# A Mamba front's B and C rows: the split remainder kept in SBUF instead of PSUM, and four due times moved

## The reference, cut to what matters

```python
xc = silu(conv(in_proj(x)));  dbl = xc @ x_proj.T           # 40 columns
dt, B, C = split(dbl)                                       # 8, 16, 16
delta = softplus(dt @ dt_w.T + dt_b)
dA = exp(delta * A);  dBu = delta * xc * B
h = dA_t * h + dBu_t;  y_t = sum_n h * C_t                  # scan over 512 tokens, 16 states
out = (y + xc * D) * silu(z) @ out_proj.T
```

## Time and profile before

| | |
|---|---|
| time, median of 3 runs | 3703.71 us (3700.42 to 3713.71) |
| the profiled execution's own time | 3700.42 us |
| its span in the profile | 3699.1 us |
| PE busy | 2934.4 us (79%) |
| DVE busy | 2480.3 us (67%) |
| ACT busy | 2005.1 us (54%) |
| POOL busy | 1625.7 us (44%) |

### The profile page before, as it was taken

One profiled execution on the slowest core, in us unless ns is written; L12 is line 12 of the kernel. 1 busy time (PEld: TensorE's weight loads), 2 busy tenths in 40 slices (PEclk: granted clock), 3 DMA queues, 4 the chain that ended last, 5 costly groups with the idle time before them and its releaser, 6 DMA issues.

```text
span 3699.1 us, 42302 instructions
## 1 busy us (share of the span) xinstructions
PE 2934.4 (79%) x15540; PEld 1347.2 (36%) x15618; DVE 2480.3 (67%) x2851; ACT 2005.1 (54%) x3613; POOL 1625.7 (44%) x1005
## 2 busy tenths in 40 slices
PE   5799988956577787878776897888768888888876
PEld 2233333421222223223223633333245555555543
DVE  3887834369988887888885332877656565666552
ACT  1465651144468677767764312666545555556543
POOL 2211101124657877776875012555544444435341
PEclk6899998966678887888787997898889999999998
DMA  3222100121112211211212000011000000000000
GB/s 87 45 42 53 29 2 0 41 60 25 35 35 57 42 40 33 62 37 36 51 34 104 1 0 12 23 23 23 12 21 11 21 21 11 21 11 21 11 21 23
DMA packets 79738, 114.43 MB, mean 31 GB/s; under 512 B 16270, under 2 KB 49422, under 8 KB 78106
## 3 DMA queue, kind: packets, MB, share of 16 engines
q1 hardware_dynamic: 68268, 103.06, 11.4%
q0 software_dynamic: 11264, 8.66, 1.8%
HBM read 37.70 MB, written 17.33 MB: 15 GB/s over the span
## 4 chain that ended last, share of the span: by engine, by line
PE 46%; DVE 23%; ACT 14%; issue 7%; POOL 6%; DMA 2%; SPq 1%; POOLq 0%; DVEq 0%; ACTq 0%
DVE layer_mamba_state L1386 7%; PE psum L1166 4%; DVE psum L1374 3%; PE psum L1239 3%; ACT layer_mamba_decay L1316 3%; PE psum L2660 3%; PE psum L826 2%; PE psum L2217 2%; PE psum L958 2%; PE psum L2731 2%; PE psum L2691 2%; DVE layer_peak L767 2%; POOL layer_qk L3052 2%; ACT L1316 1%; DVE layer_v_between L2944 1%
## 5 line engine op out<-in xcount | busy, mean ns | idle before, releaser
L1428 POOL TENSOR_TENSOR layer_mamba_state<-layer_mamba_state,layer_mamba_c 128x1024 f32<-128x1024 f32 x320 | 780.9, 2459 | 351.8 <-DVE layer_mamba_state L1386 347.9
L1386 DVE TENSOR_TENSOR_SCAN layer_mamba_state<-layer_mamba_decay,psum 128x1024 f32<-128x1024 f32 x320 | 731.4, 2286 | 43.9 <-ACT layer_mamba_decay L1316 10.3
L1239 PE MATMUL psum<-layer_mamba_state,two_to_one 128*64 128x512 f32 x1280 | 420.2, 746 | 105.0 <-DVE layer_mamba_x L1403 82.9
L1316 ACT ACTIVATE layer_mamba_decay<-layer_mamba_delta_wide,layer_weights 128x511 f32<-128x511 f32 x640 | 416.2, 711 | 60.8 <-DMA layer_mamba_delta_wide<-layer_mamba_delta 30.0
L1374 DVE TENSOR_TENSOR psum<-psum,layer_mamba_u_wide 128x1024 f32<-128x1024 f32 x320 | 393.5, 1230 | 45.2 <-PE psum L1200 19.2
L767 DVE TENSOR_REDUCE layer_peak<-psum 128x2 f32<-128x1024 f32 x256 | 308.4, 1221 | 95.3 <-PE psum L738 90.6
L839 ACT ACTIVATE layer_exps<-psum 128x1024 f32<-128x1024 f32 x256 | 255.8, 1023 | 152.5 <-PE psum L806 152.5
L2851 ACT ACTIVATE layer_p<-psum,layer_stats 128x128 f32<-128x128 f32 x512 | 180.6, 369 | 136.1 <-DVE layer_stats L2973 135.9
L3057 POOL TENSOR_TENSOR layer_p<-layer_p,layer_stats 128x512 f32<-128x512 f32 x128 | 132.5, 1039 | 255.6 <-DVE layer_stats L2980 255.3
L3044 POOL TENSOR_TENSOR layer_qk<-layer_qk,layer_v_between 128x1024 f32<-128x1024 f32 x64 | 150.5, 2351 | 189.8 <-DVE layer_v_between L2944 187.9
L1326 ACT ACTIVATE layer_mamba_c<-psum 128x512 f32<-128x512 f32 x192 | 112.9, 588 | 190.5 <-PE psum L1200 187.8
(11 more groups left out here) (366 smaller groups left out, 5995.0 us busy)
## 6 DMA issues: line engine op xcount, KB each, us to landing
layer_mamba_delta_wide<-layer_mamba_delta SPq DMA_DIRECT2D x160, 128.0 KB, 2.3
layer_mamba_u_wide<-layer_mamba_work SPq DMA_DIRECT2D x160, 128.0 KB, 2.4
layer_v_between<-layer_v SPq DMA_DIRECT2D x16, 512.0 KB, 4.3
qk_dram<-layer_qk_parts SPq DMA_DIRECT2D x16, 384.0 KB, 3.0
layer_q_rows<-qk_dram SPq DMA_DIRECT2D x96, 64.0 KB
layer_k_rows<-qk_dram SPq DMA_DIRECT2D x96, 64.0 KB
layer_v_between<-layer_v SPq DMA_DIRECT2D x16, 384.0 KB, 5.6
layer_weights<-weights_dram SPq DMA_DIRECT2D x1, 4147.0 KB, 18.1
```

What stands on the lines that cost most here:

```text
L1239: e = pe.matmul(c.psum[j * HALF:(j + 1) * HALF, self.sum_banks[h], :], c.two_to_one[:, :], self.state[i % len(self.state)][:, j, :], start ...
L1316: e = act.activation(decay[:, j, 1:SEQ], self.delta_wide[h][:, j, 1:SEQ], ACT.Exp, scale=rates[:, rate:rate + 1])
L1386: dve.tensor_tensor_scan(state, decay, self.fill.rearrange("p j t -> p (j t)"), 0.0, ALU.mult, ALU.add).then_inc(self.scanned, 1)
L1428: pool.tensor_tensor(state, state, self.both(self.c_wide[turn % self.C_BUFFERS][:, :]), ALU.mult).then_inc(self.multiplied, 1)
```

## The change

It does three things.

1. The remainder of the split goes to the first 64 rows of the SBUF tile `proj` and no longer back into the PSUM bank. The cast and the rest read it there. The split therefore also waits for `proj_kept` (the two further waits are on the unit before). The bank of the projection is free when the split is done, not when the rest is done, and the plan's `until` for it is earlier by the same step.
2. In `PLAN1` the split goes from 4.68 to 4.75, the cast from 4.82 to 4.9 and the rest from 4.95 to 5.05.
3. In `PLAN1` the delta products go from 5.06 to 4.9. `PLAN3` is not touched, but layer 3 uses the changed class.

```diff
--- before.py
+++ after.py
@@ -1177,14 +1177,14 @@
             c.bank_read[at] = self.z_gated, u * H + h + 1
         now = plan.front(u, plan.proj)
         yield now
-        at = self.banks.take(("proj", u), now, plan.front(u, plan.rest) + 0.8)
+        at = self.banks.take(("proj", u), now, plan.front(u, plan.split) + 0.8)
         hold.wait_ge(self.x_made, (u + 1) * H)
         c.wait_bank(at)
         for h in range(H):
             m = pe.matmul(c.psum[0:rows, at, :], w[name + "x_proj"][:, h * rows:(h + 1) * rows], self.x[slot][h][:, :],
                           start=h == 0, stop=h == H - 1)
         m.then_inc(self.proj_made, 1)
-        c.bank_read[at] = self.bc_split, u + 1
+        c.bank_read[at] = self.split_made, u + 1
         for h in range(H):
             now = plan.front(u, plan.dt) + 1.2 * h
             yield now
@@ -1283,7 +1283,7 @@
             act.activation(self.proj[DT_AT:rows, :], c.psum[DT_AT:rows, at, :], ACT.Copy).then_inc(self.proj_kept, 1)
             yield plan.front(u, plan.cast)
             hold.wait_ge(self.split_made, u + 1)
-            act.activation(self.bc[slot][0:2 * BC_ROWS, :], c.psum[0:2 * BC_ROWS, at, :], ACT.Copy).then_inc(self.cast_made, 1)
+            act.activation(self.bc[slot][0:2 * BC_ROWS, :], self.proj[0:2 * BC_ROWS, :], ACT.Copy).then_inc(self.cast_made, 1)
             yield plan.front(u, plan.soft)
             for h in range(H):
                 hold.wait_ge(self.u_ready[h], self.transferred(u - 1))
@@ -1340,17 +1340,19 @@
         return merged(self.dve_fronts(), self.dve_fills(), self.dve_scans(), self.dve_backs())
 
     def dve_fronts(self):
-        c, dve, hold, H, plan = self.c, self.c.dve, self.c.dve_hold, self.halves, self.plan
+        c, dve, hold, H, plan, proj = self.c, self.c.dve, self.c.dve_hold, self.halves, self.plan, self.proj
         rest, second = slice(0, 2 * BC_ROWS), slice(BC_ROWS, 2 * BC_ROWS)
         for u in range(self.units):
             slot, bc = u % 2, self.bc[u % 2]
             yield plan.front(u, plan.split)
-            proj = c.psum[:, self.banks.given["proj", u], :]
+            hold.wait_ge(self.bc_split, u)
+            hold.wait_ge(self.cast_made, u)
+            hold.wait_ge(self.proj_kept, u + 1)
             hold.wait_ge(self.bc_copied, u + 1)
-            dve.tensor_tensor(proj[rest, :], proj[rest, :], bc[rest, :], ALU.subtract).then_inc(self.split_made, 1)
+            dve.tensor_tensor(proj[rest, :], c.psum[rest, self.banks.given["proj", u], :], bc[rest, :], ALU.subtract).then_inc(
+                self.split_made, 1)
             yield plan.front(u, plan.rest)
             hold.wait_ge(self.split_made, u + 1)
-            hold.wait_ge(self.proj_kept, u + 1)
             hold.wait_ge(self.cast_made, u + 1)
             dve.tensor_tensor(bc[second, :], proj[second, :], bc[second, :], ALU.subtract).then_inc(self.bc_split, 1)
             for h in range(H):
@@ -1458,7 +1460,7 @@
 
 PLAN1 = MambaPlan(
     start=48.0, pace=8.3, item=3.75, first=0.55, spread=-4.2, c_spread=-2.8, copy=-1.8, decay=-6.0,
-    conv=((2.45, 2.63), (2.81, 2.99)), x=(2.9, 3.22), z=3.5, z_gate=3.8, proj=4.2, keep=4.5, split=4.68, cast=4.82, rest=4.95, dt=5.06,
+    conv=((2.45, 2.63), (2.81, 2.99)), x=(2.9, 3.22), z=3.5, z_gate=3.8, proj=4.2, keep=4.5, split=4.75, cast=4.9, rest=5.05, dt=4.9,
     soft=5.15, log=5.75, u=(6.15, 6.35), send_delta=(6.5, 6.6), send_u=(7.17, 7.62), multiply=3.9, sum=16.0, y=1.6, gate=1.78,
     back=2.0, out=2.3)
 ROWS_AT = [30.0, 34.0, 38.0, 42.0, 46.0, 50.0, 54.0, 58.0]
```

## The result

The changed kernel takes 3732.87 us (median of 5 runs, 3729.01 to 3736.27), the kernel before in the same comparison 3709.40 us (5 runs, 3700.42 to 3716.18). The ratio is 1.007 with a 95% interval of 1.0051 to 1.0091: slower, by about 26 us. The forecast was 3716 us in a range of 3697 to 3728: the sign held, the size didn't. The forecast started from a median of 3703.71 us for the kernel before, which is 3709.40 here; that is 5.7 of the 17 us between 3716 and 3732.87.

A forecast was written before the change was run, and what follows sets the result against it. Layer 1 was taken as bound by the chain from dt copy through delta products and ScalarE to the softplus sum. 15.5 - 2.5 - 0.6 + 0 = +12.4 us on 3700.42 gave 3712.8; with 3.3 for the median, 3716, range 3697 to 3728.

The forecast's parts named there:

- The chain and the list of waits: Layer 1: dt copy, delta products, second Abs, logarithms, softplus sum bound a unit; split, cast and rest are off it.
- The logarithm's wait: Layer 1, VectorE: the softplus sum's wait for the logarithm grows from 10.7 us to some 30.
- the three early units: Layer 1 units at 839, 930, 1027: VectorE decides, its gain would count; -0.6 us, from 0.3 in each of two.
- Layer 3: Its 8 units: split 0.6 us later, TensorE mostly carries the chain; taken as 0, between -2 and +5 us.
- the port rival: Layer 3: GpSimd wins the port and the rest waits; up to +19 us beside the forecast, 3735; chance 0.06.
- The ordinary units: Nine layer 1 units where TensorE idles until the dt rows come: 1.98 us each less 2.3 slack, +15.5 us.
- the price of the pair: Ordinary units: the sum pair between the delta products delays the second Abs by its length, 1.98 us at the low clock.
- the upper bound: Ordinary units: if the clock falls earlier and slows the delta products too, the delay per unit is 3.1 us.
- the seven other units: Layer 1 units outside the nine ordinary: three expert at -2.5 us, three early at -0.6, one starting the stage.
- the expert units: Three layer 1 units with expert products between: first delta product runs earlier; -1.0 us for two, -0.5 for the third.
- VectorE's gain: Ordinary units: VectorE gains 0.93 us each, left out of the sum because it only lengthens the wait for the logarithm.
- the clock rival: TensorE's clock falls earlier, so an ordinary unit costs 2.6 us, not 1.98: +5.6 us, 3726 with layer 3; chance 0.18.

The follow-up runs named there:

- e3: Kernel before with the remainder in SBUF and the delta products ahead (dt 4.9), split, cast and rest at their old times: 3735.47 us, ratio 1.0073.
- e10: The changed kernel run again, unaltered, for a second profile: layer 1 +23.6 us against the first profile of the kernel before.
- e9: The kernel before run again, unaltered, for a second profile: layer 1 +0.2 us against its first profile.
- e5: Changed kernel with the sum pair held back behind both delta products instead of between them: 3722.49 us, ratio 1.0044.
- e2: Kernel before with only the remainder in SBUF, with its waits and bank, all four PLAN1 times as before: 3722.08 us, ratio 1.0033.
- e6: Changed kernel with three useless z products on TensorE while it waits for the dt rows in nine ordinary units: 3730.64 us, ratio 1.0072.
- e11: Changed kernel with one useless z product between sum pair and second delta product in nine ordinary units: 3756.55 us, ratio 1.0142.
- e1: Changed kernel with only dt put back to 5.06, so the delta products stand behind the sum pair again: 3702.15 us, ratio 0.999.
- e4: Kernel before with only split, cast and rest moved (4.75, 4.9, 5.05), rest behind the fill, remainder in PSUM: 3693.07 us, ratio 0.997.

## Why the prediction was wrong

*The chain and the list of waits* were read rightly. The rest's wait is gone and worth nothing in the changed kernel (e3 against the changed kernel: 1.0073, 1.007). The logarithm's wait is 30.5 us (forecast: some 30; but my own terms, 9 x 2.91 - 2.3 on 10.7, give 34.6, so that this came out so well is partly luck). The split waits 0.67 us more (0.6) and stands on the chain only in the three early units, in two of which it stood before. Layer 3 adds 0.4 us (forecast 0), its rests take 0.68 us, so the port rival there is out.

*The ordinary units* were forecast at 15.5 us. The second Abs came later by 20.5 us over nine units, 2.27 each (forecast 1.98), the softplus sum by 18.4; until the next keep, or the stage's end, 19.8 us were left (19.1 in e10; 18.1 and 17.4 against e9, the second profile of the kernel before). The mis-sized term is the price of the pair: to its 1.98 us the lower clock of the products beside it has to be added, in part, which I had as a rival (2.6 us) and as the upper bound (3.1). e5 shows that part by itself, 3.8 us over the nine units.

*The step that failed* is the seven other units: forecast -2.5 for the expert units and -0.6 for the early ones, measured +3.8 and +3.1 in the first profile (+3.0 and +1.2 in e10; against e9, +3.5 and +4.9, and in e10 +2.7 and +3.0). In the first profile that is 10 of the 15 us missing in layer 1.

In the early units I wrote that VectorE decides and its gain would count, and gave the later Abs no price. (The third early unit, where no product is beside the rest, got no term at all.) At 930 and 1027 the sum did come 0.4 and 0.3 us earlier; why the unit at 930 is 0.9 us longer all the same I haven't traced. At 839 the chain of the changed kernel goes another way:

```profile
849.45 2.02 PE psum L1194 x2
...
858.17 1.15 ACT layer_mamba_work L1302 x2
859.32 0.49 ACT layer_mamba_c L1326
...
859.95 0.57 PE psum L1682 x2
...
860.54 0.17 DVE layer_choose_columns L1884
```

The same operation on VectorE, in the kernel before and in the changed one:

```profile
852.87 0.15 DVE L1882 TENSOR_SCALAR layer_choose_columns<-psum 128x3 f32<-128x3 f32 x1
```

```profile
860.54 0.16 DVE L1884 TENSOR_SCALAR layer_choose_columns<-psum 128x3 f32<-128x3 f32 x1 [1.99 <-PE psum L1682]
```

The late second product delays ScalarE's list up to the copy of C (L1326); behind that stands the count of the expert choice on TensorE (L1682), and VectorE stands still 1.99 us for the count where it had not waited. VectorE was busy ahead of the softplus sum, but with work that hangs on ScalarE's list too. So the 4 to 5 us by which the sum came after the logarithm were not all slack: of the Abs's 2.8 us, 1.5 reached the sum and 2.4 the next keep.

In the expert units the second Abs came 0.1 us later, 0.1 and 0.5 us earlier, where I had -1.0, -0.5 and -1.0. (In e10 the one at 1247 is 0.6 us earlier; in the first profile a slow x projection stood ahead of it.) The loss came behind the softplus, 2.4 us of it in the unit at 1465, and with it TensorE's clock was lower. The same expert products in the unit at 1465, as windows of the kernel before and of the changed one:

```profile
1504.00:1508.00 4.00, 4.00 (x25) 2.43 (x24) 3.97 (x4) 0.76 (x2) 2.54 (x2) 1.00 0.00 0
```

```profile
1523.00:1527.00 4.00, 4.00 (x14) 2.90 (x16) 3.52 (x2) 0.96 (x2) 2.54 (x2) 0.50 0.00 0
```

At 1.00 and at 0.50: the clock fell at the same place of the program (1499.3 and 1518.4); in the one the high level was back by 1503, in the other not before 1539. The unit is 2.4 and 2.3 us longer in the two profiles of the changed kernel. Over all 17 profiles the five us from 40 us behind its keep are at 0.50 in five (these two, e2, e3, e6; the unit adds 1.4 to 2.4 us) and at 0.92 or more in twelve (it adds at most 0.1; e11, with still later products, is among them). That the level is the cause is argued from this agreement, as for the unit at 1750. I had priced the clock only where the pair stands; an edit that moves work in time can also change at which level the dense stretches behind it run.

*The SBUF remainder* was priced at nothing and costs 7 to 12 us where dt is at 5.06 (e1 against e4, e2 against the kernel before). In the changed kernel I can't separate it, since the kernel before has no free bank for dt at 4.9 without it; a late logarithm hides at least the long rest at 1105. The prediction leant on the order of the starts to tell who waits. In layer 3 that held, at 1105 it didn't: the rest's record starts 0.69 us ahead of the GpSimd product's, and it was the rest that took 4.15 us. GpSimd's starts are rough in a profile, so this is a reading and not a rule. *VectorE's gain* was rightly left out of the sum, but only because the move of dt buries it: without that move the later rest is worth 11 us (e4), by a path that stays open. Two small slips change nothing: from the second Abs to the first logarithm's end it is 7.21 us, not 7.26, and with layer 3 at its upper end the clock rival adds up to +23, not +22.

What stays open: why e5 and e6 gain 22 and 12 us in layer 1 of their profiles and only 10 and none in the medians. The changed kernel's profiled execution was 7.2 us slower than its median and e6's 7.4 us faster, which goes some way for e6 and not for e5. One profile of each can't tell. And no run moves dt while it leaves all PSUM banks as they were; e5 keeps the changed kernel's banks and loses most of the excess in layer 1, which speaks against them.

## What to carry to other kernels

Before moving an operation ahead of another, look at what the queue puts *between* its two halves: here one pair of small matmuls in the gap of a two-product chain was paid nine times, 2.27 us each for a pair of 1.98. A wait that is removed on an engine off the chain was worth nothing here once the same edit lengthened the chain; taken alone (the rest behind the fill, the remainder left in PSUM) it gave 11 us. A profile is one execution: compare its own time with the median before its stages are read against a ratio. And before calling an engine's lateness slack, follow what its earlier work was released by.

## What the runs showed of the hardware

- TensorE's granted clock isn't a property of the stage. The four x projection records took 1.96 us or 3.74 us at the same place of the same program (e10 and the first profile), and the expert unit at 1750 was 5.0 to 6.5 us longer in the four profiles in which the granted clock over its products was 0.50 to 0.57, and at most 1.4 us longer in the thirteen where it was 0.86 or more.
- A VectorE operation with both inputs in SBUF (0.68 us alone) took 4.15 us in e1. It began at 1106.89, ahead of the GpSimd product whose record begins at 1107.58 but behind the start of the descriptor instruction at 1106.51, and ended 0.55 us after that product. The three other long rests of e1 (1.23, 1.29 and 1.98 us) also ended 0.55 to 0.57 us after a GpSimd product.
